# Two attentions of a decoder: both parts of V in one stationary block, and weight loads, output products and a query tile placed anew

## The reference

```python
# first: 16 heads of 32
q, k, v = (heads(x @ W.T) for W in (Wq, Wk, Wv))
w = softmax(q @ k.T / sqrt(32) + causal)
x + (w @ v) @ Wo.T
# second: 32 query heads of 64 in 8 groups, one key and value head per group
y = rmsnorm(x) * rms_w
q, k, v = split(y @ w_in.T); q, k = rope(q), rope(k)
w = softmax(causal(q @ k.T * 64 ** -0.5))
x + (x_in + (w @ v) @ w_out.T)
```

## Time and profile before

| | |
|---|---|
| median of 3 runs | 2130.75 us (2122.9 to 2133.69) |
| the profiled execution, own time | 2136.04 us |
| its span | 2134.7 us |
| TensorE, granted clock over the span | 0.936 |
| busy, PE / PEld | 1889.3 us (89%) / 1632.2 us (76%) |
| busy, VectorE / ScalarE / POOL | 1129.9 (53%) / 788.8 (37%) / 967.3 us (45%) |
| the 384 matmuls on VL (L149) | 126.2 us busy, 329 ns each |
| bank 7 emptied | 40 ScalarE copies, 595 ns; 40 VectorE low parts, 691 ns |

### The profile page before, as it was taken

The page is one execution under the profiler, slowest core; times in us unless marked ns, Lnnn a source line. Parts: engine busy times, 40 slices in busy tenths (PEclk is TensorE's granted clock), DMA queues, the critical chain, the costliest instruction groups (busy, mean ns, idle before and its releaser), DMA issues. The chain is left out here.

```text
span 2134.7 us, 30662 instructions
## 1 busy us (share of the span) xinstructions
PE 1889.3 (89%) x10274; PEld 1632.2 (76%) x10274; DVE 1129.9 (53%) x2767; ACT 788.8 (37%) x2029; POOL 967.3 (45%) x926
## 2 busy tenths in 40 slices
PE   5788979878999999899569999999998999897896
PEld 4676867657899898799447888888877788785795
DVE  4555685437333333235746666666665656455344
ACT  2554643231222222121146556565553423212231
POOL 2332341248782759813736546455453101006584
PEclk8899999999999999899789999999999999789998
DMA  2434531025663446431533333233321110002565
GB/s 88 134 110 137 159 135 67 1 88 203 230 203 120 154 161 220 157 118 51 157 77 91 85 85 101 60 89 83 79 66 46 60 45 1 20 1 96 174 205 195
DMA packets 102630, 232.33 MB, mean 109 GB/s; under 512 B 18752, under 2 KB 19008, under 8 KB 99408
## 3 DMA queue, kind: packets, MB, share of 16 engines
q1 hardware_dynamic: 82736, 144.89, 22.8%
q0 software_dynamic: 19744, 85.47, 12.1%
HBM read 126.23 MB, written 57.93 MB: 86 GB/s over the span
## 5 line engine op out<-in xcount | busy, mean ns | idle before, releaser
L631 POOL TENSOR_SCALAR a_E<-a_E,a_inv 128x128 f32<-128x128 f32 (+3 forms) x384 | 218.9, 588 | 278.1 <-DVE a_inv L752 278.1
L149 PE MATMUL bank<-f_UH,f_XH 128*128 x596 | 202.2, 339 | 19.8 <-POOL f_UL L161 14.8
L664 ACT ACTIVATE a_E<-a_E,a_top 128x512 f32<-128x512 f32 (+3 forms) x384 | 211.1, 567 | 8.4 <-DVE a_top L746 8.3
L746 DVE CUSTOM_DVE_ANT_0 a_E<-a_causal,bank 128x512 f32<-128x512 bf16 (+3 forms) x384 | 164.2, 482 | 73.3 <-PE bank L897 45.9
L149 PE MATMUL bank<-f_UH,f_XL 128*128 x596 | 194.6, 327 | 0.0
L149 PE MATMUL bank<-f_UL,f_XH 128*128 x596 | 194.6, 326 | 0.0
L656 ACT ACTIVATE a_PHL<-bank 128x512 fp32r<-128x512 f32 (+1 forms) x288 | 131.2, 528 | 156.0 <-PE bank L913 156.0
L149 PE MATMUL bank<-a_PHL,a_VH 128*128 128x512 f32 (+3 forms) x768 | 186.7, 332 | 0.3 <-DVE a_QL L161 0.3
L161 DVE TENSOR_TENSOR a_PHL<-bank,a_PHL 128x512 fp32r<-128x512 f32 (+1 forms) x288 | 153.8, 587 | 29.7 <-ACT a_PHL L656 29.6
L1603 DVE TENSOR_TENSOR f_gate<-bank,f_gate 128x352 f32<-128x352 f32 x79 | 41.3, 523 | 215.9 <-PE bank L149 215.9
L149 PEld LDWEIGHTS bank<-a_PHL,a_VH 128*128 128x128 f32 x768 | 140.3, 196 | 16.3 <-DVE a_QL L161 0.6
(11 more groups left out here) (389 smaller groups left out, 4976.2 us busy)
## 6 DMA issues: line engine op xcount, KB each, us to landing
f_uraw<-f_up POOLq DMA_DIRECT2D x18, 1408.0 KB, 6.5
f_xb<-table SPq DMA_DIRECT2D x86, 256.0 KB, 3.1
table<-f_ob SPq DMA_DIRECT2D x86, 256.0 KB, 2.3
table<-a_zeros SPq DMA_DIRECT2D x31, 512.0 KB, 4.3
f_draw<-f_down POOLq DMA_DIRECT2D x27, 512.0 KB, 4.5
a_g<-a_f SPq DMA_DIRECT2D x160, 64.0 KB, 2.0
a_raw<-a_qkv SPq DMA_DIRECT2D x36, 256.0 KB, 3.1
f_uraw<-f_up POOLq DMA_DIRECT2D x9, 704.0 KB, 4.8
```

Of the source, the lines that this page charges most:

```text
L149: m = pe.matmul(out, a, b, start=first and i == 0 and j == 0, stop=last and i == n - 1 and j == 2, skip_group_check=not check)
L631: e.tensor_scalar(self.E[sl][:, a], self.E[sl][:, a], self.inv[:, sl, i:i + 1], 0.0, ALU.mult, ALU.add).then_inc(*self.s_nrm.up(N, m - 1, i))
L664: x = e.activation(E, E, ACT.Exp, scale=-1.0, bias=self.top[:, sl, i:i + 1], accum_out=self.total[:, sl, i:i + 1])
L746: e.tensor_tensor_reduce(self.E[sl][:, self.E_AT[i]:self.E_AT[i] + w], self.causal[:, T - w:T], bank[:, off:off + w], -1.0, HUGE, ALU.add, ...
```

## The change

V gets one tile instead of two. In a head's 128x128 block the high part stands in the head's own columns and the low part in the columns half a block (64) away (`across`), so one pass of the probabilities gives the head's rows of the high part in its own half of the bank and those of the low part in the other half. Two matmuls remain for each block: V x PH and V x PL. As both halves are used, the heads are taken in two groups (`half`): heads 0, 1 and 2, 3 in a0, each head by itself in a1. Bank 7 is started and emptied for each group: ScalarE copies the group's 64 rows to QH, VectorE takes their low part to QL and then adds the other 64 rows to it, after a wait for itself. The new low x low product is computed as well. V is cleared in a0 only, and once.

```diff
-        self.VH, self.VL = sb("VH", [heads, NT, P], F32R), sb("VL", [heads, NT, P], F32R)
+        self.V = sb("V", [heads, NT, P], F32R)
+        self.across = [slice((h * hd + P // 2) % P, (h * hd + P // 2) % P + hd) for h in range(heads)]
+        self.half = heads // 2
+        self.rows = [slice(0, P // 2), slice(P // 2, P)]
...
-            self.FILL = [[("P", K, 1)], [("P", 0, 1)], [("P", V, 1)], [("T", 1)] + [("O", g, -1) for g in range(TT, NT)],
-                         [("P", K, 0, 1)], [("P", 0, 0, 1)], [("P", V, 0, 1)],
-                         [("T", 0, 1)] + [("O", g) for g in range(TT)]]
-            self.SPLIT = {2: (K, 1), 3: (0, 1), 4: (V, 1), 5: (self.wt, 0)}
+            self.FILL = [[("P", K, 1), ("O", 2, -1), ("O", 3, -1)], [("P", 0, 1)], [("P", V, 1)],
+                         [("O", 4, -1), ("O", 5, -1), ("T", 1)],
+                         [("P", K, 0, 1), ("O", 6, -1), ("O", 7, -1)], [("P", 0, 0, 1)], [("P", V, 0, 1)],
+                         [("O", 0), ("O", 1), ("T", 0, 1)]]
+            self.SPLIT = {2: (K, 1), 3: (0, 1), 5: (V, 1), 6: (self.wt, 0)}
+            self.LEAD = {K: 3, 0: 4, V: 2, self.wt: 2}
...
-                         [("O", 6, -1), ("O", 7, -1)], [("P", 3, 1)], [("P", V, 1)], [("T", 1), ("P", 0, 1)],
-                         [("P", 1, 1)], [("P", 2, 1)], [("P", K, 0, 1)], [("O", 0), ("O", 1)], [("O", 2), ("O", 3)],
-                         [("P", 3, 0, 1)], [("P", V, 0, 1)], [("T", 0, 1), ("P", 0, 0, 1)]]
+                         [("P", 3, 1)], [("O", 6, -1), ("O", 7, -1)], [("P", V, 1)], [("T", 1), ("P", 0, 1)],
+                         [("P", 1, 1)], [("P", 2, 1)], [("P", K, 0, 1)], [("O", 0), ("O", 1)], [("P", 3, 0, 1)],
+                         [("O", 2), ("O", 3)], [("P", V, 0, 1)], [("T", 0, 1), ("P", 0, 0, 1)]]
+            self.LEAD = {}
...
+        self.loads = {}
+        for m in [self.begin - 1] + list(self.loops):
+            for x in self.split(m):
+                self.loads.setdefault(m - (self.LEAD.get(x[1], 1) if m >= 0 else 1), []).append(x)
...
-        for z in (self.VH, self.VL):
-            e.memset(z[:, :, :, :].bitcast(F32), 0.0)
+        if self.heads > 2:
+            e.memset(self.V[:, :, :, :].bitcast(F32), 0.0)
...
-            if 3 <= m < self.M + 3 and self.jobs[m - 3][3] == self.heads - 1:
+            if 3 <= m < self.M + 3 and self.jobs[m - 3][3] % self.half == self.half - 1:
...
-                e.activation(self.QH[:, r, b * T:b * T + T], self.k.bank[self.OB][:, :], ACT.Copy).then_inc(
+                e.activation(self.QH[own, r, b * T:b * T + T], self.k.bank[self.OB][own, :], ACT.Copy).then_inc(
...
+        low = self.QL[own, r, b * T:b * T + T]
+        e.wait_ge(*self.s_ohi.after(N, j, r, b, g))
+        low_part(e, low, bank[own, :], self.QH[own, r, b * T:b * T + T]).then_inc(*self.k.d.up())
+        e.wait_ge(*self.k.d.now())
+        e.tensor_tensor(low, bank[other, :], low.bitcast(F32), ALU.add).then_inc(*self.s_olo.up(N, j, r, b, g))
...
+                e.matmul(out, self.V[:, h, at, :], self.PH[m % 2][:, a], start=first and sblk == 0, stop=False)
+                t = e.matmul(out, self.V[:, h, at, :], self.PL[m % 2][:, a], start=False, stop=last and ci == 2)
```

More of the change, by code:

```diff
@@ L566, in sp @@
         for m in self.loops:
-            for x in self.split(m + 1):
+            for x in self.loads.get(m, []):
                 self._load(x)
@@ L769, in dve, with _dve_low_rows @@
                 self.norm.dve_rest(NT + m)
-            if 3 <= m < self.M + 3 and self.jobs[m - 3][3] == self.heads - 1:
-                j, b, r, h = self.jobs[m - 3]
-                a = slice(b * T, b * T + T)
-                e.wait_ge(*self.s_ohi.after(N, j, r, b))
-                low_part(e, self.QL[:, r, a], self.k.bank[self.OB][:, :], self.QH[:, r, a]).then_inc(
-                    *self.s_olo.up(N, j, r, b))
+            if 3 <= m < self.M + 3 and self.jobs[m - 3][3] % self.half == self.half - 1:
+                self._dve_low_rows(*self.jobs[m - 3])
+    def _dve_low_rows(self, j, b, r, h):
+        e, N, g, bank = self.k.dve, self.name, h // self.half, self.k.bank[self.OB]
+        own, other = self.rows[g], self.rows[1 - g]
+        low = self.QL[own, r, b * T:b * T + T]
[3 more added lines that the diff above has]
+        e.tensor_tensor(low, bank[other, :], low.bitcast(F32), ALU.add).then_inc(*self.s_olo.up(N, j, r, b, g))
     def _dve_rotate(self, x):
@@ L923, in _pe_values @@
             e.wait_ge(*self.s_vlo.after(N, j, b))
-        if h == 0 and self.OB in emptied:
+        first, last = h % self.half == 0, h % self.half == self.half - 1
+        if first and self.OB in emptied:
             e.wait_ge(*emptied[self.OB])
@@ L928, in _pe_values @@
             for sblk, _ in chunk:
-                a = slice(self.P_AT[sblk], self.P_AT[sblk] + T - sblk * P)
-                t = product(e, self.k.bank[self.OB][:, sblk * P:T],
-                            [(self.VH[:, h, b * TT + sblk, :], self.VL[:, h, b * TT + sblk, :])],
-                            [(self.PH[m % 2][:, a], self.PL[m % 2][:, a])],
-                            first=h == 0 and sblk == 0, last=h == self.heads - 1 and ci == 2)
+                a, at = slice(self.P_AT[sblk], self.P_AT[sblk] + T - sblk * P), b * TT + sblk
+                out = self.k.bank[self.OB][:, sblk * P:T]
+                e.matmul(out, self.V[:, h, at, :], self.PH[m % 2][:, a], start=first and sblk == 0, stop=False)
+                t = e.matmul(out, self.V[:, h, at, :], self.PL[m % 2][:, a], start=False, stop=last and ci == 2)
         t.then_inc(*self.s_av.up(N, m))
-        if h == self.heads - 1:
-            emptied[self.OB] = self.s_olo.after(N, j, r, b)
+        if last:
+            emptied[self.OB] = self.s_olo.after(N, j, r, b, h // self.half)
     def end(self):
```

16 lines of the change are left out of this document (9 added, 7 removed).

## The result

The changed kernel takes 2101.48 us (median of 4 runs, 2093.11 to 2104.44) against 2127.32 us for the kernel before beside it (4 runs): a ratio of 0.987, 95% interval 0.9845 to 0.9895. It is faster, by 26 us where 78 were forecast, and it lies 9.5 us above the upper end of the range.

The account below looks back on a forecast made before the run. It took a1 as near TensorE's bound and a0 as held up by late weight loads and a bank shared with V's transpose. 2136 - 54 (a0) - 27 (a1) = 2055 us, forecast as a 2053 median, range 2028 to 2092.

Parts of the forecast that it names:

- the sum for SP: a0's half step: K's low part at 6.07 us, 24 transfers 0.63 apart, clearing 0.6, 1.43 to the scores: 23.5 us.
- The first half: a0's first half step: its transfers start no sooner but lose a load among them, -2 us.
- the last loops lose 0.62 each, and late emptyings give some back: -1: End of a0: each last loop shortens by 0.62 us, partly offset by late emptyings, -1 us in all.
- Tile 0's chain: a1, from the start of query tile 0's projecting loop to the scores of n = 2 or 10: 24.55 us becomes 22.8.
- From n = 2 on: 8.2 + 9.1 + 6.6 + 9.1 + 6.5 = 39.5: Rest of a1's half step after tile 0's chain: 39.5 us, making the half 62.3 us, 4 less than now.
- the 0.5 us in a0: a0's half step: 0.5 us added because the first output product must wait for a longer emptying.
- 96 x 0.62 = 60 us of TensorE, 40 in a1: Two passes instead of three: 96 heads each save 0.62 us of TensorE at the high clock, 60 us, 40 in a1.
- A: a1 gives nothing, the operations before the next maxima eating TensorE's gain: 2082 us, or 2095 with a second low-clock loop; chance 0.16.
- B: a0 gives half: transfers and banks hold its half step at 29 us, 2079 us in all; chance 0.10.
- D: Slower: a1's projecting loops become VectorE's and ScalarE's, 81.4 us a half, 2201 us; sign: a_QL waits before values products; chance 0.03.
- C: a1 comes near TensorE's bound because emptying 64 rows costs 0.3 us: another -27, 2028 us; chance 0.06.
- E: a0's loads come no sooner, SP waiting for a free raw slot: 2095 us, with A nearly no gain; chance 0.05.

Follow-up runs that it names:

- run 12: The whole change without VectorE's addition of the other half's rows, against the kernel before: ratio 0.9689; a0 247.9 us, a1 560.1 us.
- the ladder: From new fill tables and early loads in three passes, adding emptying by halves, then the addition, then removing the third pass: a1 572.1, 577.2, 610.1, 591.3 us.
- Run 6: Three passes with the new fill tables and early loads, plus emptying by halves and VectorE's addition, against the kernel before: 2122.36 us, ratio 0.9973; a1 610.1 us.
- the placing alone: The kernel before with only the new fill tables and early loads of both attentions, three passes and one emptying a tile: 2076.82 us, ratio 0.9745.
- run 11: The whole change with a1's query tile 0 projected one loop earlier and later splits, against the kernel before: ratio 0.9927, a1 607.4 us.
- run 15: The two-pass kernel without the addition, with the earlier query tile 0 and later splits, against the kernel before: ratio 0.9729, a1 573.0 us.

## Why the prediction was wrong

**The bounds that I read held.** a0 was held up by loads and by the bank shared with V's transpose; with both gone TensorE works almost without a gap in five of six half steps. The raw-weight waits of ScalarE and TensorE's waits for V's low parts are gone, the emptying operations took 0.59 and 0.69 us, 384 matmuls are gone.

**a0, forecast -54, measured -40.7.** The half steps went from six of 33.5 us to six of 26.0 (68.11 to 224.18 us; the rows are the starts of the loops 4, 24 and 28, counted over the whole stage):

```profile
68.11 0.79 PE L913 MATMUL bank<-a_KS,a_QS 96*128 96x512 f32 x1 [4.95 <-DMA a_QS<-a_g]
...
198.13 0.50 PE L913 MATMUL bank<-a_KS,a_QS 96*128 96x512 f32 x1 [3.57 <-DMA a_QS<-a_g]
...
224.18 0.40 PE L913 MATMUL bank<-a_KS,a_QS 96*128 96x512 f32 x1
```

That is -44.7 where I had -51; five of the six are at 24.6 to 26.05, and the one that ends at 198.13 takes 29.0, with a wait of 3.57 us at its end for the next query tile. In that half step SP also issues two loads for the next stage (`m_craw`, at 184.24) ahead of the query's transfers, which the sum for SP left out; the last of those transfers is issued by 194.21, 3.9 us before the scores, where I had put 1.43. The addition is not the cause, since without it (run 12) the same half step takes 28.7; what delays the landing was not tried. The first half gave 1.6 where I had 2. The step that failed most is "the last loops lose 0.62 each, and late emptyings give some back: -1": the tail grew from 36.9 to 42.5 us, +5.6. There the values products have no projection ahead of them, and waits of up to 2.3 us for L794 stand before them and before the output products (the waits of a0 above; 6.8 of those 9.7 us lie in the tail). Without the addition the tail is 37.1 (run 12). Together 6.3 + 0.4 + 6.6 = 13.3 us, of which the addition accounts for 8 (run 12). Two sums of a0 were slightly off without any effect: SP's terms add up to 23.2 and not 23.5, and four loops without the pass at 0.62 make 15 of the 54 us and not 12.

**a1, forecast -27, measured +3.4.** The half was to be 62.3 us and is 66.6 (1124.37 to 1524.01, six halves; the table at the ladder has both by loops). Tile 0's chain was 1.1 us too short: 22.8 forecast, 23.2 to 24.2 measured, with 3 to 3.9 us of waiting where I had said 3. The step that failed is the other one: "From n = 2 on: 8.2 + 9.1 + 6.6 + 9.1 + 6.5 = 39.5". It measures 41.7 to 45.2, 42.7 on average. In it I let TensorE never wait, though the output products of n = 3 and 11 need the last emptying, which now ends one operation later: that loop takes 9.35 to 14.16 us instead of 9.1, on average 10.7. Together n = 2 and 3 were to take 17.3 us; they take 18.85 in five of six half steps, and 22.3 in the one with the loop of 14.16. Loop n = 2 runs 8.1 to 9.5 instead of 8.2, and n = 6 takes 7.2 to 8.5 instead of 6.5, with a wait for a residual add (0.69 us at 1313.04 above). Sums of busy loops cannot show this. I had asked who waits for the emptying at the values product alone, and priced the addition at two places, tile 0's chain and the 0.5 us in a0. Run 6 prices it at 33 us in a1 in three passes, and run 12 at 31 in two. Without it a1 takes 560.1 us, 27.8 less than before: my -27 is the time of a kernel in which the addition costs nothing.

**The saving was oversized too.** "96 x 0.62 = 60 us of TensorE, 40 in a1" holds loop by loop where TensorE waits for nothing: such loops went from 7.07 to 6.43 us and from 9.75 to 9.13. A whole step of a1 should have lost 10 us by it, and its busy time fell by 5.4 to 7.2, since some of the rest ran at the lower clock. In time it brought 27 (run 6 to the whole change), and in a1 no more than 2.5 us in a step even without the addition (run 12 against the placing alone). The same two passes that I had credited with 12 of a0's 54 us are, with the emptying that they bring, a loss of 5 there.

**The rivals.** A (a1 gives nothing) is what happened in a1. Its 2082, and with the second low-clock loop its 2095, which lay above the end of my own range, become 2095 and 2108 with the 13 us that a0 fell short. The execution took 2104, but not by A's sum: a1 took 3 us more than before, and some 5 us came from stages whose code did not change. I had it at 0.16, because "the other loops have slack": they did not where an output product waits. B had a0's right direction and the wrong place, but for one half step of 29. D's sign, waits for a_QL ahead of values products in a1, is there with 3.5 us in three waits. Its mechanism, VectorE late, is what TensorE waits for in two passes once the query tile is early (runs 11 and 15), but at some 65 to 69 us a half (129.4 us a step in run 15; 344.28 us for the five halves from 1234.65 in run 11), far from its price of 81.4. C and E fell: 0.69 us, and no late loads. And one case was missing from the list: A with part of B. I had treated them as alternatives, though one cause, the third operation on the bank, drives both: all of a1's loss against the forecast and 8 of a0's 13 us (run 12).

**What a better kernel is.** The placing alone, in three passes: 0.9745 (0.9715 to 0.9775). With the later splits, with or without the earlier query tile, 0.973 and 0.9732; the intervals do not tell the three apart.

## What to carry to other kernels

A saving on an engine near its bound is worth at most the gap between the stretch and the next engine's or chain's own time. Where a rewrite takes matmuls off TensorE and gives each result one more operation to pass through before its bank and its tile are free, list everyone who waits for that result, and price the operation at each of them, not only at the next user of the bank. Run the parts of a combined change apart: here the part that was meant to help TensorE cost 24 us, and dropping it is worth nearly as much again as the whole change saved.

## What the runs showed that I had not expected

**Rows cost nothing, operations do.** An operation that empties 64 rows of a bank takes what 128 rows take: 0.59 us on ScalarE and 0.69 on VectorE, so that to empty by halves doubles the price.

**VectorE stands at each emptying, but that alone costs nothing.** The low parts of the emptyings in one step of a1, VectorE: busy us, mean ns and the idle time before them: after (16 in the step), with the addition in three passes, and with the placing alone.

```profile
L161 DVE TENSOR_TENSOR a_QL<-bank,a_QH 64x512 fp32r<-64x512 f32 x16 | 11.0, 688 | 16.2 <-ACT a_QH L690 16.2
```
```profile
L161 DVE TENSOR_TENSOR a_QL<-bank,a_QH 64x512 fp32r<-64x512 f32 x16 | 11.0, 688 | 22.8 <-ACT a_QH L692 22.8
```
```profile
L161 DVE TENSOR_TENSOR a_QL<-bank,a_QH 128x512 fp32r<-128x512 f32 x8 | 5.5, 692 | 14.6 <-ACT a_QH L686 14.5
```

Before, 8 of them waited 5.1 us in all. VectorE stands at each emptying until the values product and ScalarE's copy are done, with the next maxima behind it. With the placing alone 8 of them wait 14.6 us, in a kernel that is faster than both of the others, so the length of this wait is no price.

**VectorE's elementwise product takes longer when it starts behind GpSimd's.** After, first VectorE's rotation in two loops, then GpSimd's:

```profile
1211.79 0.69 DVE L801 TENSOR_TENSOR a_f<-a_f,a_cos_sin 128x512 f32<-128x512 f32 x1 [0.17 <-DMA a_g<-a_f]
...
1220.86 1.79 DVE L801 TENSOR_TENSOR a_f<-a_f,a_cos_sin 128x512 f32<-128x512 f32 x1
```
```profile
1211.84 1.79 POOL L635 TENSOR_TENSOR a_g<-a_g,a_cos_sin 128x512 f32<-128x512 f32 x1 [5.76 <-DMA a_g<-a_f]
...
1220.39 1.71 POOL L635 TENSOR_TENSOR a_g<-a_g,a_cos_sin 128x512 f32<-128x512 f32 x1 [4.28 <-DMA a_g<-a_f]
```

Where VectorE starts first it takes 0.69 us; where it comes 0.47 us behind GpSimd, 1.79. Before, it came first: 692 ns on average in a step, now 1374. Ten of these make 6.8 us, about what my 17 us of busy time lacked. Most of it takes the place of a wait: where VectorE starts first it then waits 1.25 us for GpSimd's product, and its addition follows 1.95 us after its product's start, against 1.82 in the other order.

**The low clock costs less than the loop that it lengthens.** After the wait of 3.19 us above, the next matmuls of 512 columns started 0.23 us apart only at first, then 0.43 (granted clock 0.81 from 1289.00 to the end of the loop). In the whole change each wait of about 3 us or more ahead of n = 2 or 10 is followed by such a loop, of 8.1 to 9.5 us. In run 12 waits of 2.4 to 2.7 us stand there, and two of six are followed by a loop at the full clock. Two half steps of run 12, first the scores of n = 10 and the starts of n = 11 and 12, then the same of n = 2, 3 and 4:

```profile
1305.47 0.50 PE L914 MATMUL bank<-a_KH,a_QH 128*128 128x512 f32 x1 [2.49 <-DMA a_QL<-a_g]
...
1312.00 0.40 PE L914 MATMUL bank<-a_KH,a_QL 128*128 128x512 f32 x1
...
1323.07 0.40 PE L914 MATMUL bank<-a_KH,a_QH 128*128 128x512 f32 x1
```
```profile
1367.59 0.50 PE L914 MATMUL bank<-a_KH,a_QH 128*128 128x512 f32 x1 [2.38 <-DMA a_QL<-a_g]
...
1375.73 0.40 PE L914 MATMUL bank<-a_KH,a_QL 128*128 128x512 f32 x1
...
1385.18 0.40 PE L914 MATMUL bank<-a_KH,a_QH 128*128 128x512 f32 x1
```

Loop n = 10 takes 6.53 us at a granted clock of 1.00 and the next 11.07; loop n = 2 takes 8.14 at 0.79 and the next 9.45: 17.6 us both times. In the whole change n = 2 and 3 together take 18.8 to 18.9 us in five of the six half steps, whether n = 2 takes 8.12 or 9.50. A wait for the emptying, ahead of the output products, is longer where n = 2 is shorter, so that the clock of n = 2 makes no difference there; only where the clock falls a second time, in the loop of 14.16 us, does it show: 22.3.
